# Two attention layers on one core: when values, masks and the turn of the maxima are issued

## The reference

```
x = layernorm(x + attention0(x))       # 16 heads of 8, scores minus |i-j|, causal
x = layernorm(x + mixture(x))          # one of 8 experts per token
x = layernorm(x + attention1(x))       # 16 heads of 64, gated position bias, causal
x = layernorm(x + gated_mlp(x))

attention: out[i] = sum_j softmax_j(q[i].k[j] * scale + bias[i,j], j <= i) v[j]
```

## Time and profile before

| | |
|---|---|
| median of 3 runs | 2235.26 us (2231.14 to 2236.41) |
| profiled execution | 2221.2 us, its span 2219.4 us |
| TensorE busy in it | 2040.5 us (92%) |
| VectorE, ScalarE, GpSimd busy | 1351.3, 1148.5, 841.2 us |
| first attention | from some 20 to 545 us |
| second attention | from about 1020 to 1850 us |
| a group of the first | 28.87 us |
| a group of the second | 25.26 us |

### The profile page before, as it was taken

One profiled execution on the slowest core, in us unless ns is written; L12 is line 12 of the kernel. 1 busy time (PEld: TensorE's weight loads), 2 busy tenths in 40 slices (PEclk: granted clock), 3 DMA queues, 4 the chain that ended last, 5 costly groups with the idle time before them and its releaser, 6 DMA issues.

```text
span 2219.4 us, 34339 instructions
## 1 busy us (share of the span) xinstructions
PE 2040.5 (92%) x11728; PEld 1162.8 (52%) x11728; DVE 1351.3 (61%) x3316; ACT 1148.5 (52%) x1859; POOL 841.2 (38%) x544
## 2 busy tenths in 40 slices
PE   5799999998587998896999999999999999999998
PEld 2333333333486554553566665656656555656644
DVE  4788888884732777874666676666666664333311
ACT  2366666667343686782455555555555553223222
POOL 5000000001501455442677777777777772000000
PEclk8799999999688999996999999999999999999999
DMA  5233333112275689896666777667776687533300
GB/s 180 100 125 121 127 131 130 60 51 74 97 197 142 207 263 332 265 294 162 153 155 163 177 177 177 156 161 180 173 175 163 157 226 210 116 86 86 91 5 10
DMA packets 260300, 335.88 MB, mean 151 GB/s; under 512 B 22732, under 2 KB 181756, under 8 KB 259720
## 3 DMA queue, kind: packets, MB, share of 16 engines
q1 hardware_dynamic: 244824, 305.82, 51.5%
q0 software_dynamic: 7664, 24.39, 3.0%
q10 hardware_dynamic: 7640, 3.48, 0.6%
HBM read 193.69 MB, written 122.62 MB: 143 GB/s over the span
## 4 chain that ended last, share of the span: by engine, by line
PE 41%; issue 6%; DVE 4%; SPq 2%; DMA 1%; ACT 0%; DVEq 0%
PE ps L1287 10%; PE ps L956 6%; PE ps L940 6%; PE ps L909 6%; PE ps L941 5%; PE ps L1238 2%; DVE a1mx L1012 2%; PE ps L1298 1%; PE ps L1275 1%; PE ps L1276 1%; PE ps L943 1%; DVE a1mx L1008 1%; SPq L1162 1%; DMA a1FQ<-s_q 1%; DVE a1mx L1005 0%
## 5 line engine op out<-in xcount | busy, mean ns | idle before, releaser
L1123 POOL TENSOR_TENSOR a1sum<-a1sum,a1prob 128x1024 f32<-128x1024 f32 (+3 forms) x256 | 462.9, 1808 | 82.6 <-ACT a1prob L1066 50.3
L1066 ACT ACTIVATE a1prob<-ps 128x512 f32<-128x512 f32 (+2 forms) x640 | 327.9, 553 | 243.8 <-PE ps L943 209.8
L479 DVE TENSOR_REDUCE a0grid<-ps 128x8 f32<-128x1024 f32 x288 | 351.1, 1223 | 102.1 <-PE ps L351 64.7
L1005 DVE CUSTOM_DVE_ANT_0 ps<-ps,c_mask_ij 128x128 f32<-128x128 f32 x496 | 264.3, 551 | 195.1 <-issue 190.8
L580 ACT ACTIVATE a0prob<-ps 128x1024 f32<-128x1024 f32 x288 | 286.0, 1024 | 168.4 <-PE ps L377 110.9
L940 PE MATMUL ps<-a1QA,a1KA 69*128 69x512 f32 (+3 forms) x768 | 284.6, 378 | 4.4 <-DMA a1QA<-a1neg 4.4
L956 PE MATMUL ps<-a1prob,a1V 128*64 128x512 f32 (+3 forms) x1536 | 273.1, 498 | 4.5 <-ACT a1prob L1066 4.5
L941 PE MATMUL ps<-a1QB,a1KB 128*128 128x512 f32 (+3 forms) x768 | 263.3, 350 | 0.0
L909 PE MATMUL ps<-a1KA,a1QA 68*128 68x128 f32 x744 | 224.7, 381 | 4.8 <-DMA a1KA<-s_g 3.9
L956 PEld LDWEIGHTS ps<-a1prob,a1V 128*64 128x64 f32 x1536 | 102.8, 138 | 172.1 <-issue 138.2
L1008 DVE TENSOR_REDUCE a1mx<-ps 128x1 f32<-128x320 f32 x248 | 145.9, 588 | 70.5 <-PE ps L909 67.6
(11 more groups left out here) (269 smaller groups left out, 3105.1 us busy)
## 6 DMA issues: line engine op xcount, KB each, us to landing
a1FQ<-s_q SPq DMA_DIRECT2D x128, 256.0 KB, 7.9
a1KB<-s_k SPq DMA_DIRECT2D x128, 256.0 KB, 8.6
s_xs<-c_zero POOLq DMA_DIRECT2D x19, 1024.0 KB, 9.4
s_q<-mqkT SPq DMA_DIRECT2D x32, 512.0 KB, 3.6
s_v<-mv SPq DMA_DIRECT2D x32, 512.0 KB, 5.8
s_k<-a1KH SPq DMA_DIRECT2D x32, 512.0 KB, 5.0
s_k<-a1KL SPq DMA_DIRECT2D x32, 512.0 KB, 5.9
a1KA<-s_k SPq DMA_DIRECT2D x64, 256.0 KB
```

Source lines behind the costliest of these rows:

```text
L479: dve.tensor_reduce(grid[g % 2][:, :, a:b + 1:b - a], banks(("max", k)), axis=AX.X, op=ALU.max).then_inc(s1_free, 1)
L1005: dve.tensor_tensor_reduce(bank[:, 0:w], bank[:, 0:w], const["mask_ij"][:, BANK - w:BANK], 1.0, LOWEST, ALU.add, ALU.max, mx[:, x % 2, h, ...
L1066: act.activation(weights_of(g, u)[:, group[0]:group[-1] + 1, off:BANK], both(e, u, group), ACT.Exp).then_inc(weighed, 1)
L1123: pool.tensor_tensor(t[:, :, off:BANK], t[:, :, off:BANK], weights_of(g, u)[:, :, off:BANK], ALU.add).then_inc(summed, 1)
```

## The change

First attention:
- The 12 rows of values become 18 units of values, the same units as the exponentials'. A unit is one product of 256 columns per head, or two of 128 where its blocks have different keys or where one block of queries is opened and the other is not. The table `visits` says in which step they are made, two steps or more behind their exponential. Steps 2 and 8 have none, steps 9 and 10 two each.
- `units1` is cut differently: masks stand in four units with two masked blocks each (four products more narrow, two of them twice), instead of four units with one and two with two. Their positions are 3, 8, 12 and 14. Two units on the second diagonal have no mask.
- The copies of `O` move from units 9 and 4 to 7 and 1, their transposes from 16 and 6 to 10 and 4, the divisions likewise.

Second attention:
- In a unit with a bank for each head, both masks come behind both heads' products.
- The turn of the maxima moves from behind the three maxima of unit 8 to behind the values of the second run, for groups 1 to 30 in the place of its making; the negation and the row's DMA move with it.

```diff
-    units1 = [((t, j), (t, j + 1)) for t in range(IT) for j in range(0, t, 2)] + [((t, t), (t + 2, t + 2)) for t in range(0, IT, 4)]
+    units1 = [((t, j), (t, j + 1)) for t in range(IT) for j in range(0, t - 1, 2)] + [((t, t - 1), (t + 2, t + 1)) for t in range(1, IT, 4)]
+    for n, t in zip((3, 8, 12, 14), (0, 1, 4, 5)):
+        units1.insert(n, ((t, t), (t + 2, t + 2)))
...
-    after = {1: ((9,), ()), 2: ((10,), ()), 3: ((11,), ()), 5: ((), (0,)), 6: ((), (1,)), 7: ((), (2,)), 8: ((), (3,)),
-             10: ((), (4,)), 11: ((), (5,)), 13: ((), (6,)), 15: ((), (7,)), 17: ((), (8,))}
...
+    visits = {3: (0,), 4: (1,), 5: (2,), 6: (3,), 7: (4,), 9: (5, 6), 10: (7, 8), **{u + 2: (u,) for u in range(9, NU)}}
...
-                for h in range(H):
-                    end = pe.matmul(O[h * WIDE:(h + 1) * WIDE, off:BANK], V[:, g // per * IT + j, (g % per * H + h) * COL:(g % per * H + h) * COL + WIDE],
-                                    prob[:, h, mine[0]:mine[-1] + 1, :], start=j == 0, stop=r == CLOSE[c])
+                alone = j != j2 or opens[c, t] != opens[c2, t2] and u in (opens[c, t], opens[c2, t2])
+                parts = [(j, t, slice(a, a + 1)), (j2, t2, slice(b, b + 1))] if alone else [(j, t, slice(a, b + 1))]
+                for key, query, some in parts:
+                    off = (query - c * TILES) * P
+                    for h in range(H):
+                        end = pe.matmul(O[h * WIDE:(h + 1) * WIDE, off:off + P * (some.stop - some.start)],
+                                        V[:, g // per * IT + key, (g % per * H + h) * COL:(g % per * H + h) * COL + WIDE], prob[:, h, some, :],
+                                        start=u == STRETCH[c][0] and some.start == a, stop=u == STRETCH[c][-1] and some.stop == b + 1)
...
-                if u == 4 and g > 0:
+                if u == 1 and g > 0:
                     copy_out(g - 1, 1)
-                if u == 9 and g < GROUPS:
+                if u == 7 and g < GROUPS:
                     copy_out(g, 0)
...
-        if u == TURN and g + 1 < G:
-            found.append(("turn", g + 1, 0))
...
+            if r == 1 and 0 < g < G - 1:
+                order.append(("turn", g + 1, 0))
...
-                    if diag:
-                        last = pe.matmul(both(e, u, group)[:, :, 0:P], const["identb"][:, :],
-                                         const["mask_ji_add"][:, :].unsqueeze(1).to_broadcast([P, len(group), P]), start=False, stop=True)
-                    last.then_inc(scored, 1)
+                    if not diag:
+                        last.then_inc(scored, 1)
+
+                for e, group in places(g, u) if diag else ():
+                    pe.matmul(both(e, u, group)[:, :, 0:P], const["identb"][:, :],
+                              const["mask_ji_add"][:, :].unsqueeze(1).to_broadcast([P, len(group), P]), start=False, stop=True).then_inc(scored, 1)
...
-                    if u == turn_after(g) + 1 and g + 1 < G:
+                    if u == (TURN if g > 0 else TURN + 2) and g + 1 < G:
                         row(g + 1)
```

More of the change, by code:

```diff
@@ L63, in attention0 @@
         units2 += [((c, a[i], a[k]), (c, a[i2], a[k2])) for i, k, i2, k2 in ((0, 0, 1, 1), (0, 1, 0, 2), (0, 3, 2, 3), (1, 2, 1, 3), (2, 2, 3, 3))]
[L64 removed]
+    NB = len(blocks2)
     NU = NB // 2
     assert len(units1) == len(units2) == NU
[L67 removed]
     LEAD = NU + 6
[L69 to L75 removed]
+    STRETCH = [[u for u in range(NU) if units2[u][0][0] == c] for c in range(HALF)]
+    opens = {(c, t): min(u for u in STRETCH[c] if (c, t) in [(x[0], x[2]) for x in units2[u]]) for c in range(HALF) for t in range(c * TILES, (c + 1) * TILES)}
+    visits = {3: (0,), 4: (1,), 5: (2,), 6: (3,), 7: (4,), 9: (5, 6), 10: (7, 8), **{u + 2: (u,) for u in range(9, NU)}}
+    assert [u for s in visits for u in visits[s]] == list(range(NU)) and all(u + 2 <= s for s in visits for u in visits[s])
     TOTAL = GROUPS * NU
@@ L86, in attention0 @@
         turns += [("out", g - 1, 1)] if g > 0 else []
+        turns += [("out", g, 0)] if g < GROUPS else []
         turns += [("max", g + 1)] if g + 1 < GROUPS else []
-        turns += [("out", g, 0)] if g < GROUPS else []
     turn_at = {x: n for n, x in enumerate(turns)}
@@ L357, in maxima @@
                             end = pe.matmul(half(x, m)[:, :, a, :], Q[g % 2][r:r + ROWS, query * P:(query + 1) * P], BK[g % 2][r:r + ROWS, :, key * P:(key + 1) * P],
-                                            start=a == 0, stop=False)
+                                            start=a == 0, stop=a == 1 and t2 != j2)
                 if t2 == j2:
@@ L441, in tensor_program @@
                     turn_maxima(k // NU - 1)
-                if k > LEAD:
-                    g, u = divmod(k - 1 - LEAD, NU)
-                    if u in after:
-                        for r in after[u][0] if g > 0 else ():
-                            values(g - 1, r)
-                        for r in after[u][1] if g < GROUPS else ():
-                            values(g, r)
                 if k < LEAD:
@@ L452, in tensor_program @@
                 g, u = divmod(k - LEAD, NU)
+                for group, step in ((g - 1, u + NU), (g, u)):
+                    if 0 <= group < GROUPS:
+                        for v in visits.get(step, ()):
+                            values(group, v)
                 if g < GROUPS:
                     scores(k - LEAD)
-                if u == 6 and g > 0:
+                if u == 4 and g > 0:
                     turn_out(g - 1, 1)
-                if u == 16 and g < GROUPS:
+                if u == 10 and g < GROUPS:
                     turn_out(g, 0)
@@ L577, in exponentials @@
                 if g > 0:
-                    act.wait_ge(p_free, NR * (g - 1) + max(in_turn.index(rows.index(x[:2])) for x in units2[u]) + 1)
+                    act.wait_ge(p_free, NU * (g - 1) + u + 1)
                 a, b = (blocks2.index(x) for x in units2[u])
@@ L977, in tensor_program @@
                             values(g, u)
+                    if r == 1 and 0 < g < G - 1:
+                        job(d)
+                        d += 1
         def places(g, u):
@@ L1037, in vector_program @@
                         d += 1
+                    if u == 2 * TILES - 1 and 0 < g < G - 1:
+                        job(d)
+                        d += 1
                 if g % PAIRS == 1 and g > 1:
```

20 lines of the change are left out of this document (9 added, 11 removed).

## The result

| | before | after |
|---|---|---|
| median | 2233.2 us (2230.93 to 2236.41, 4 runs) | 2209.14 us (2204.84 to 2213.37, 4 runs) |
| ratio, with its 95% interval | | 0.9893 [0.9875, 0.991] |
| profiled execution | 2221.2 us | 2213.4 us |
| a group of the first attention | 28.85 us | 28.17 us |
| a group of the second attention | 25.27 us | 24.67 us |

24 us went, 23.3 were forecast (2212 us). The group times are medians from one turn of the maxima to the next.

The account below looks back on a forecast made before the run. TensorE was taken to bound both attentions. First attention minus 7.5, its tail minus 1.3, turn minus 8 and masks minus 6.5 sum to minus 23.3 us, taken off the median 2235.26: 2212 us, range 2198 to 2232.

Parts of the forecast that it names:

- First attention: Steady groups: fewer TensorE waits outweigh added work, 28.87 to 28.37 us a group, minus 7.5 us over 16 groups.
- the remaining waits: First attention: 1.8 us a group of TensorE waiting left out of 3.1, mostly 0.57 each behind steps 2 and 8.
- The work term: First attention: values in more pieces and changed products and masks give TensorE 0.8 us more to do a group.
- The tail: End of the first attention: TensorE's two waits for the copy of O, 0.68 and 0.63, go: minus 1.3 us.
- Now the next values stand two steps behind the copy: End of the first attention: the reason given why TensorE's waits for the copy of O go, minus 1.3 us.
- Turn: Second attention: moving the turn removes 0.39 and costs 0.12, net 0.27 us a group, minus 8 us over 30 groups.
- Nothing, if the change from values to products hides it: Second attention: lower bound of the turn's cost at its new place, priced at 0.12 us, upper bound 0.28.
- D: Rival, chance 0.03: second attention's turn gives its gain back, its late negation delaying the third maxima product; minus 15, 2220 us.
- Masks: Second attention, units with a bank per head: both masks last gain 0.05 us each unit, minus 6.5 us over 128 units.
- A: Rival, chance 0.18: first attention gains nothing and pays every piece, masks give nothing, only the turn stays; 2232 us.
- B: Rival, chance 0.22: second attention's masks and turn work, the first attention is flat; minus 15, 2220 us.
- C: Rival, chance 0.07: first attention slower by a ceiling on TensorE's instruction starts, 52 ns each; 2324 us.

Follow-up runs that it names:

- e10: Changed kernel with the second attention's late masks before values, and the first's transposes (maxima and copies of O) behind values: 0.9883 of the kernel before.
- e2: Kernel before with only the second attention's turn of the maxima moved behind the second run's values: ratio 0.9933 to the kernel before, second group 24.88 us.
- e1: Kernel before with only the second attention's masks moved behind both heads' products: ratio 0.9976 to the kernel before, second group 25.06 us.
- e4: Kernel before with only the first attention changed, the second as before: ratio 0.9973 to the kernel before, first group 28.20 us.
- e8: Changed kernel with all pieces of values 128 columns wide, 36 a group instead of 25: ratio 0.9872 to the kernel before, first group 28.23 us.
- e3: Kernel before with both second attention edits, masks and turn, the first attention as before: ratio 0.9908 to the kernel before, second group 24.67 us.

## Why the prediction was right, and where it wasn't

**First attention: mechanism right, terms off both ways.** Forecast was 28.37 a group, found 28.17. Two pieces take 0.57 as said, idle time is 0.86 (under 1.2 as said), and M waits behind steps 2 and 8, by 0.47 each where 0.57 was said. The mis-sized term is the remaining waits: 1.8 were kept, 0.3 of them only because the arithmetic missed the trace of before by 0.27. Without that correction the forecast would have been 28.1. The work term, plus 0.8, can only be estimated: where TensorE sat idle, the spacing beyond the usual one came to some 3.0 us of a group before, in six places and not the prediction's eight, and to 1.2 in three places after (0.47, 0.47 and the 0.28 of step 13). That fell by 1.8 and the group by 0.7, so all the rest, the work and the small delays of plain steps, cost some 1.1. The saving is 0.68 a group instead of 0.5: 8.1 us between the turns, 7.5 forecast.

**The tail: wrong sign.** Forecast minus 1.3, found plus 1.0. "Now the next values stand two steps behind the copy" was the step that failed. TensorE in the last group:

```profile
515.47 0.40 PE L382 MATMUL ps<-a0BQ,a0K 51*128 51x256 f32 x4
516.32 0.65 PE L401 MATMUL ps<-a0prob,a0V 128*32 128x128 f32 x16 [0.46 <-ACT a0oT L588]
...
535.94 0.65 PE L401 MATMUL ps<-a0prob,a0V 128*32 128x128 f32 x16 [0.55 <-ACT a0prob L581]
```

```profile
514.66 1.02 ACT L581 ACTIVATE a0prob<-ps 128x1024 f32<-128x1024 f32 x1 [0.33 <-PE ps L334]
515.59 0.59 ACT L588 ACTIVATE a0oT<-ps 128x512 f32<-128x512 f32 x1
```

Between the last values ahead of a copy (from 514.56 on, 0.57) and the next values there stand only two S without M (0.34 and 0.39). The values would start at 515.86, but ScalarE first ends an exponential (1.02) and then copies (0.59). The waits for the copy stayed, 0.46 each at 516.32 and 523.03, where 0.68 and 0.63 were. And a wait came up that no term held: before, the last four rows of values stood together behind everything (2.36 us); now the last unit's values wait for the last exponential, 0.55 at 535.94. The whole tail has 0.6 more idle time (30.6 - 26.91 against 29.6 - 26.53) and 0.4 more work. The prediction moved a wait by counting steps, and had their lengths without M before it. The loss of 1.0 is no matter of one execution: from the last turn to the last transposes 29.3 us pass in every run with values by unit (28.7 in e10), and 28.3 in every run with values by row.

**Turn: right, and one term too large.** 0.39 a group went (e2), 0.27 was forecast. The wait of 0.27 and the 0.12 at the old place both went; the 0.12 set for the new place is 0.01. "Nothing, if the change from values to products hides it" was the end of the range that held. That the turn lies inside what this change of kind costs anyway is the likely reading; the runs show its price, not the reason. So the turn gave 12 us, the forecast's own bound, instead of 8. D is excluded: the three maxima products behind the turn, from 1413.43 on, have no idle time ahead of them.

**Masks: right.** 0.05 each, by e1 and by the rows. The second mask came 0.07 behind the first, 0.05 to 0.10 given. The rule of the Trainium skill (TensorE: Matmul & The Clock Gate, Part 2, step by step), by which the prediction put the gain at 0.08 each, does not come out in time: e1 measured 0.05. The load engine sat idle 0.28 and loaded the first mask only as that mask began (1413.33, both rows); the second mask's load did run under the first mask, and yet was not free. Whether these loads go to the background buffer, on which the rule depends, no run here shows.

**The sum.** From turn to turn and in the tail 24.1 went, 23.3 were forecast: 8.1 - 1.0 = 7.1 instead of 8.8 in the first attention, 17.0 instead of 14.5 in the second. That the sum agrees within 1 us is partly luck: the tail and the turn were wrong in opposite directions. A fell with e1, e4 and e8, B with e4 and the groups, C with e8, D with e2.

## What to carry to other kernels

On a saturated engine, read the distance from one start to the next beside busy time: of the 0.60 us a group in the second attention 0.48 stood in no idle time. Put an odd small operation where the kind changes anyway, and like ones together, but try each place, since the same mask costs 0.04 us ahead of maxima and 0.21 ahead of values. Two moves that come to nothing apart can gain together when one makes the gaps into which the other puts its work (here minus 0.24 and plus 0.30 apart, minus 0.68 together). And when the last work of a stage is cut finer, look at its end by itself: there the next group's work, which fills waits in the steady groups, is missing.

## What the runs showed that was not expected

- VectorE's addition for the next group's queries (L1021 before, L1027 after) grew from a median of 1466 ns to 1991 ns, both between 1204 and some 2200, with its code unchanged; VectorE's busy time of the second attention rose by 39 us, and nobody waited for it. It comes from the masks' order: with the masks alone moved (e1) the median was 1708 ns, with the turn alone (e2) 1494, with both (e3) 2000. The likely reason, that it now overlaps GpSimd's sums at other points, was not tested.

```profile
L1027 DVE TENSOR_TENSOR a1QB<-a1FQ,a1QB x62: 1204/1991/2101, 1018.2 to 1788.6; 64x1024 fp32r<-64x1024 f32 x62
```

- The granted clock in the stretch before the second attention's steady groups differs between executions, 0.69 and 0.57 above, and that stretch takes 41 or 48 us. A saving of 5 us can't be read from two spans; it can from the groups, nearly all of which repeat within 0.05 us.
- A product of values costs its columns and nothing for being short, as long as its like stands before it: 88 more matmuls of 128 columns, with their loads, cost 0.06 us together (e8).
